# The recurrence's array of terms: from term innermost to key index innermost

## The chip, the cores and the metric

One core of a Trainium2 chip runs the whole program. The time is device time in microseconds (us) of one execution, and the lower the better. Its engines are TensorE (PE: matmuls, with PEld for weight loads), VectorE (DVE), ScalarE (ACT), GpSimd (POOL) and SyncE (SP), which mostly issues DMAs. They run side by side and wait for each other by semaphores.

## What is computed

A block of six parts on 8 sequences of 512 tokens with 128 features: a routed expert layer, six layers of windowed attention, the expert layer again, an attention block with a two-expert mixture, a recurrence over the tokens, and the attention block with its mixture again. The change lies in the recurrence alone. For each batch and each of 16 heads it carries a state `S` of 8 x 8 numbers (key index by value index) through the 512 tokens:

```python
def step(S, inp):
    qt, kt, vt, at, gft = inp
    bs1 = jnp.einsum('bhk,bhkv->bhv', kt, S)
    S1 = S + at[..., :, None] * bs1[..., None, :]
    S2 = jnp.exp(gft)[..., None] * S1
    bs2 = jnp.einsum('bhk,bhkv->bhv', kt, S2)
    S3 = S2 + at[..., :, None] * bs2[..., None, :] + kt[..., :, None] * vt[..., None, :]
    o = jnp.einsum('bhk,bhkv->bhv', qt, S3)
    return (S3, o)
```

Of the outputs `o` only those of the last 176 tokens are used.

## The kernel before

8 batches x 16 heads are 128 states, one on each partition. A state is 8 x 8 float32 words on its partition, value index `v` outside, key index `k` innermost. `SH` is a ring of 8 such states. VectorE runs the recurrence alone, token after token, with the keys, factors and values of 128 tokens (a chunk) in `KW`, `UA`, `FT`, `VT`.

The first 336 tokens, whose outputs nobody asks for, are taken two at a time: `pair`, 168 times. Their new state is the sum of seven 8 x 8 terms: the old state times a factor (term 0), four products of a vector of `UA` with a vector of `Z2` (terms 1 to 4), and two outer products of values and keys (terms 5 and 6). The order on VectorE is: L2808 multiplies the state with four key vectors into `M2`; L2811 writes term 0; L2814 sums `M2` over the key index into `Z2`; L2815 writes terms 5 and 6; L2820 writes terms 1 to 4; L2824 sums the seven terms into the new state in `SH`. The terms lie in `J2` (in the tensor `fw1`), 64 x 7 words with the term innermost.

The other 176 tokens are taken one at a time, with three terms in `MJ` (64 x 3 words, the term innermost): L2875 multiplies the state with two key vectors into `M1`, L2879 makes the state times its factor (`FS`), L2882 sums `M1` into `XY`, L2884 writes term 0 (`FS` plus the outer product `KV`), L2887 writes terms 1 and 2, L2846 (`outer`) prepares the next token's `KV`, and L2895 sums the three terms into the new state. After every 8 tokens L2903 and L2906 make the 8 outputs.

An instruction on VectorE waits for an earlier one only where the program says so (`dve.wait_ge`, or `chain.link`, which waits for the instruction just added): L2814 waits for L2808, L2820 for L2814, L2824 for L2820, and the next step for L2824 (semaphore `R.step`); L2887 waits for L2882, L2895 for L2887 (not for L2846 behind it).

While the pairs run, TensorE and ScalarE work on experts and projections of the later batches. VectorE does small parts for these at fixed tokens of a chunk (`beside`): the bank sum L2731 and statistics L2227 behind tokens 28 and 86, the gates L2748 behind tokens 54 and 108, the key lengths L2754 behind token 123. In the last 176 tokens there is ever less of that, and TensorE comes to rest.

Other lines named below: L2526 to L2529 and L2657 belong to the routing of tokens to experts (`upto` is 8 experts x 32 tiles; L2528 multiplies it with `chosen`, which lies tiles by experts, and L2529 sums it over the experts); L2797 and L2799 belong to the preparation of pairs, and L2799 writes `key[:, :, 0]`, runs of 8 words 16 apart; L1723 on TensorE is the last matmul that L2731 needs.

Of the kernel before, what the change touches and what calls it, by code (L numbers as in the profile page):

```python
# [20 lines left out]
ALU = mybir.AluOpType  # L21
ACT = mybir.ActivationFunctionType
AX_X = mybir.AxisListType.X

P = 128
# [3 lines left out]
HEADS, HD = 16, 8  # L29
# [420 lines left out]
def build(nc, d, out):  # L450
    ctx = ExitStack()
    with ctx:
        def sb(name, shape, dt=F32):
            return ctx.enter_context(nc.sbuf_tensor(name, shape, dt))
# [20 lines left out]
        fw1 = sb("fw1", [P, HID])  # L475
# [37 lines left out]
        at = [0]  # L513

        def take(*shape):
            n = int(np.prod(shape))
            v = arena[:, at[0]:at[0] + n]
            at[0] += n
            assert at[0] <= 34048
            if len(shape) == 2:  # L520
                v = v.rearrange("p (a b) -> p a b", b=shape[1])
            if len(shape) == 3:
                v = v.rearrange("p (a b c) -> p a b c", b=shape[1], c=shape[2])
            return v
# [79 lines left out]
        UA = [take(CH, 2, HD) for _ in range(2)][::-1]  # L604
# [3 lines left out]
        FT, VT = ([take(CH, HD) for _ in range(2)] for _ in range(2))  # L608
        stk, stv, stq, stf = (take(TOKENS) for _ in range(4))
        KV = take(2, HD, HD)  # L610
        FS = take(HD, HD)
        MJ = take(HD * HD, 3)
        SH = take(STEP_RING, HD, HD)
        M1 = take(2 * HD, HD)
        XY = take(2, HD)
# [9 lines left out]
        scaled = [take(TOKENS) for _ in range(2)]  # L625
        N2, RN, T1 = (frow[:, k, :] for k in range(3))
        C1 = LG[:].rearrange("p a b -> p (a b)")[:, 0:CH]
        J2 = fw1[:, 32:32 + 7 * HD * HD].rearrange("p (a r) -> p a r", r=7)
        F2 = OQ.rearrange("p t v k -> p (t v k)").rearrange("p (n k) -> p n k", k=HD)
        at[0] = junk_at  # L630
        K2 = take(CH // 2, 2, HD)
# [4 lines left out]
        Z2 = take(4, HD)  # L636
# [44 lines left out]
        R = RecurrencePhase(sem)  # L681
# [1536 lines left out]
        def _(dve):  # L2218
            chain = Chain(dve, v_chain)
# [515 lines left out]
            def recurrent_experts():  # L2735
# [22 lines left out]
                def prepare(c):  # L2758
                    q = c % 2
                    wide = lambda a: a.unsqueeze(2).broadcast_to([P, R.CHUNK, HD])  # L2760
                    kn, wv, ua, av = KW[q][:, :, 0, :], KW[q][:, :, 1, :], UA[q][:, :, 0, :], UA[q][:, :, 1, :]
                    dve.wait_ge(R.rn_ready, c + 1)
                    chain.link(dve.tensor_tensor(kn, KT, wide(RN), ALU.mult))
                    chain.link(dve.scalar_tensor_tensor(out=av, in0=kn, scalar=-1.0, in1=wide(G1[q]), op0=ALU.mult,
                                                        op1=ALU.mult))
                    chain.add(dve.tensor_tensor(wv, kn, FT[q], ALU.mult))
                    chain.link(dve.tensor_tensor(ua, av, FT[q], ALU.mult))
                    chain.link(dve.tensor_tensor(KT, kn, ua, ALU.mult))
                    chain.link(dve.tensor_reduce(C1, KT, AX_X, ALU.add))
                    chain.link(dve.tensor_tensor(KT, av, wide(C1), ALU.mult))  # L2770
                    chain.link(dve.tensor_tensor(ua, ua, KT, ALU.add))
                    if R.pairs(c):
                        join_pairs(c)
                    dve.engine_nop().then_inc(R.pre_done, 1)
# [28 lines left out]
                def pair(c, at):  # L2803
                    q, n, t = c % 2, at // 2, R.CHUNK * c + at
                    s, new = SH[:, (t - 1) % STEP_RING], SH[:, (t + 1) % STEP_RING]
                    four = [P, 4, HD, HD]
                    dve.wait_ge(R.step, t + 1)
                    chain.add(dve.tensor_tensor(  # L2808
                        M2.rearrange("p (a v) k -> p a v k", a=4), s.unsqueeze(1).broadcast_to(four),
                        KW[q][:, at:at + 2].rearrange("p b a k -> p (b a) k").unsqueeze(2).broadcast_to(four), ALU.mult))  # L2810
                    chain.add(dve.tensor_tensor(J2[:, :, 0].rearrange("p (v k) -> p v k", k=HD), s,  # L2811
                                                F2[:, n].unsqueeze(1).broadcast_to([P, HD, HD]), ALU.mult))
                    dve.wait_ge(v_chain, chain.value() - 1)
                    chain.add(dve.tensor_reduce(Z2.rearrange("p a b -> p (a b)"), M2, AX_X, ALU.add))  # L2814
                    chain.add(dve.tensor_tensor(  # L2815
                        J2[:, :, 5:7].rearrange("p (v k) r -> p r v k", k=HD),
                        VT[q][:, at:at + 2].unsqueeze(3).broadcast_to([P, 2, HD, HD]),
                        K2[:, n].unsqueeze(2).broadcast_to([P, 2, HD, HD]), ALU.mult))
                    dve.wait_ge(v_chain, chain.value() - 1)
                    chain.link(dve.tensor_tensor(  # L2820
                        J2[:, :, 1:5].rearrange("p (v k) r -> p r v k", k=HD),
                        UA[q][:, at:at + 2].rearrange("p b a k -> p (b a) k").unsqueeze(2).broadcast_to(four),
                        Z2.unsqueeze(3).broadcast_to(four), ALU.mult))
                    dve.tensor_reduce(new.rearrange("p v k -> p (v k)"), J2, AX_X, ALU.add).then_inc(R.step, 2)  # L2824

                def beside(c, at):

# [32 lines left out]
                for t in range(TOKENS):  # L2860
                    c, at = divmod(t, R.CHUNK)
                    if at == 0:
                        prepare(c)
                    if at < 2 * R.pairs(c):
                        if at % 2 == 0:
                            pair(c, at)
                        beside(c, at)
                        continue
                    if at == 2 * R.pairs(c):
                        chain.link(outer(t))  # L2870
                    j = t % STEP_RING
                    s = SH[:, (j - 1) % STEP_RING]
                    new = SH[:, j]
                    dve.wait_ge(R.step, t + 1)
                    chain.add(dve.tensor_tensor(  # L2875
                        M1.rearrange("p (a v) k -> p a v k", a=2),
                        s.unsqueeze(1).broadcast_to([P, 2, HD, HD]),
                        KW[c % 2][:, at].unsqueeze(2).broadcast_to([P, 2, HD, HD]), ALU.mult))
                    chain.add(dve.tensor_tensor(  # L2879
                        FS, s, FT[c % 2][:, at].unsqueeze(1).broadcast_to([P, HD, HD]), ALU.mult))  # L2880
                    dve.wait_ge(v_chain, chain.value() - 1)
                    chain.add(dve.tensor_reduce(XY.rearrange("p a b -> p (a b)"), M1, AX_X, ALU.add))  # L2882
                    dve.wait_ge(v_chain, chain.value() - 1)
                    chain.add(dve.tensor_tensor(  # L2884
                        MJ[:, :, 0].rearrange("p (v k) -> p v k", k=HD), FS, KV[:, t % 2], ALU.add))
                    dve.wait_ge(v_chain, chain.value() - 1)
                    chain.add(dve.tensor_tensor(  # L2887
                        MJ[:, :, 1:3].rearrange("p (v k) r -> p r v k", k=HD),
                        UA[c % 2][:, at].unsqueeze(2).broadcast_to([P, 2, HD, HD]),
                        XY.unsqueeze(3).broadcast_to([P, 2, HD, HD]), ALU.mult))  # L2890
                    products = chain.value()
                    if at < last:
                        chain.add(outer(t + 1))
                    dve.wait_ge(v_chain, products)
                    dve.tensor_reduce(new.rearrange("p v k -> p (v k)"), MJ, AX_X, ALU.add).then_inc(R.step, 1)  # L2895
                    if t >= R.QUERIES and j == STEP_RING - 1:
                        if at == j or t == R.QUERIES + j:
                            dve.wait_ge(R.q_in, 32 * (c - 1))
                        seen = slice(t - R.QUERIES - j, t - R.QUERIES + 1)
                        first = max(R.CHUNK * c, R.QUERIES)  # L2900
                        asked = QD[c][:, :, t - j - first:t + 1 - first]
                        dve.wait_ge(R.step, t + 2)
                        chain.link(dve.tensor_tensor(  # L2903
                            OQ, SH, asked.rearrange("p k t -> p t k").unsqueeze(2)
                            .broadcast_to([P, STEP_RING, HD, HD]), ALU.mult))
                        chain.link(dve.tensor_reduce(OD[:, :, seen].rearrange("p v t -> p t v"), OQ, AX_X, ALU.add))  # L2906
                    beside(c, at)
# [16 lines left out]
            for b in range(2):  # L2924
                dve.wait_ge(R.rows_rstd, 1)
                dve.wait_ge(R.y_done, b + 1)
                for i in range(TPB):
                    t = TPB * b + i
# [71 lines left out]
```

## Time and profile before

| | us |
|---|---|
| timed runs, median of 3 | 5263.96 |
| timed runs, lowest to highest | 5259.31 to 5264.52 |
| span of the profiled execution | 5330.8 |

The page gives the profiled execution's own time as its span; it lies 66.8 us above the median of the timed runs. In the rows below, L12 is line 12 of the kernel, an engine's busy time leaves out its waiting, and a duration runs from the start of an instruction to its end, which may lie behind the start of the next one on the same engine. `arena` is the big tile in which most of the named arrays lie (`M2`, `MJ`, `SH`, `KW` and so on), `fw` the one in which `J2` lies.

### The profile page before, as it was taken

The numbers are of one execution on the slowest core, as the hardware profiler recorded it, in microseconds if no ns is written. First come the engines' busy times: TensorE is split into PE (matmuls) and PEld (weight loads), VectorE is DVE, ScalarE is ACT, GpSimd is POOL, SyncE is SP. The second block draws the span as 40 slices with busy tenths as digits, with TensorE's granted clock in tenths as the row PEclk, the third lists the DMA queues.
The fourth block names the chain that finished last, engine by engine and source line by source line (L and its number), as shares of the span: only waits on it lengthen the run. The fifth ranks groups of instructions, "written<-read, shape, count | busy, mean of one in ns | idle before, by whom it ended". The sixth has DMA issues, their size and how long they took to land.

```text
span 5330.8 us, 114063 instructions
## 1 busy us (share of the span) xinstructions
PE 4408.5 (83%) x43126; PEld 2610.7 (49%) x43126; DVE 3292.6 (62%) x14115; ACT 2603.4 (49%) x5100; POOL 1823.8 (34%) x3734
## 2 busy tenths in 40 slices
PE   3779999999999999984669999788770069999999
PEld 3634555555555555543633446455540034446777
DVE  3177777777777777754047772399899957772111
ACT  0336777777777777761324553444440024553333
POOL 3055666666666666662223221000000022220000
PEclk9879999999999999995768998888885568997999
DMA  3600000000000000001511000100100000000000
GB/s 95 163 11 4 2 12 2 2 12 2 6 8 2 12 2 6 2 2 30 165 29 41 1 1 1 25 13 13 31 17 17 0 12 1 1 1 3 5 5 7
DMA packets 125108, 101.75 MB, mean 19 GB/s; under 512 B 22384, under 2 KB 103568, under 8 KB 124560
## 3 DMA queue, kind: packets, MB, share of 16 engines
q1 hardware_dynamic: 119952, 85.00, 5.8%
q0 software_dynamic: 4608, 9.45, 0.8%
q8 instruction: 343, 5.62, 0.4%
q14 instruction: 205, 1.68, 0.1%
HBM read 74.56 MB, written 19.86 MB: 18 GB/s over the span
## 4 chain that ended last, share of the span: by engine, by line
PE 58%; DVE 19%; ACT 7%; POOL 7%; issue 5%; another core or an unknown queue 1%; DMA 1%; SPq 0%; POOLq 0%; DVEq 0%; ACTq 0%; PEldq 0%
PE ps L1746 6%; PE ps L1738 6%; PE ps L1317 5%; PE ps L1357 5%; PE ps L1302 4%; PE ps L1502 4%; PE ps L1514 4%; PE ps L1278 3%; PE ps L1288 3%; PE ps L1543 2%; PE ps L1187 2%; ACT arena L1928 2%; ACT arena L1910 2%; PE ps L1231 2%; DVE arena L2824 2%
## 5 line engine op out<-in xcount | busy, mean ns | idle before, releaser
L2294 DVE CUSTOM_DVE_ANT_0 arena<-ps,mask_win 128x256 f32<-128x256 f32 (+1 forms) x3072 | 1009.3, 387 | 258.5 <-PE ps L1302 256.7
L1910 ACT ACTIVATE arena<-ps 128x512 f32<-128x512 f32 (+1 forms) x1536 | 752.0, 543 | 567.6 <-PE ps L1317 558.5
L1317 PE MATMUL ps<-arena 32*64 32x384 f32 (+2 forms) x6144 | 743.8, 478 | 74.2 <-ACT arena L1910 73.8
L1302 PE MATMUL ps<-arena 32*64 32x192 f32 (+2 forms) x12288 | 696.6, 324 | 14.4 <-DVE arena L2294 13.8
L1746 PEld LDWEIGHTS ps<-w,arena 128*128 128x128 f32 x4096 | 545.1, 195 | 266.3 <-issue 223.4
L2174 ACT ACTIVATE arena<-ps,eb 128x512 f32<-128x512 f32 x512 | 352.2, 689 | 547.0 <-PE ps L1738 546.9
L2467 DVE CUSTOM_DVE_ANT_0 arena<-ps,mask_cau 128x512 f32<-128x512 f32 (+3 forms) x1024 | 446.7, 487 | 255.3 <-PE ps L1502 252.9
L2027 ACT ACTIVATE arena<-ps 128x512 f32<-128x512 f32 (+2 forms) x768 | 363.1, 526 | 463.9 <-PE ps L1514 463.7
L1746 PE MATMUL ps<-w,arena 128*128 128x128 f32 x4096 | 551.7, 279 | 26.4 <-ACT arena L2174 26.4
L990 POOL TENSOR_SCALAR_AFFINE_SELECT arena<-arena 128x1024 f32<-128x1024 f32 x384 | 420.9, 1096 | 395.4 <-ACT arena L1910 393.8
L1738 PE MATMUL ps<-arena,w 128*128 128x512 f32 x1024 | 535.3, 606 | 0.4
L1302 PEld LDWEIGHTS ps<-arena 32*64 32x64 f32 x12288 | 380.7, 134 | 271.1 <-DVE arena L2294 94.5
L1514 PE MATMUL ps<-arena 32*128 32x512 f32 (+2 forms) x1536 | 487.5, 622 | 25.4 <-ACT arena L2027 25.4
L1502 PE MATMUL ps<-arena 32*128 32x512 f32 (+3 forms) x2048 | 426.1, 518 | 22.2 <-DVE arena L2467 16.8
L1357 PE MATMUL ps<-arena 128*32 128x256 f32 (+1 forms) x6144 | 389.0, 372 | 15.4 <-POOL arena L995 15.4
L1042 POOL TENSOR_SCALAR_AFFINE_SELECT arena<-arena 128x512 f32<-128x512 f32 (+1 forms) x192 | 154.3, 805 | 708.8 <-ACT arena L2027 708.4
L2718 DVE SCALAR_TENSOR_TENSOR X<-ps,C,X 128x128 f32<-128x128 f32 x320 | 90.1, 345 | 469.9 <-PE ps L1746 469.9
L995 POOL TENSOR_SCALAR_AFFINE_SELECT arena<-arena 128x1040 f32<-128x1040 f32 (+1 forms) x384 | 343.0, 893 | 26.3
L1187 PE MATMUL ps<-ident,arena 128*128 128x128 f32 x912 | 170.7, 318 | 180.7 <-DVEq L2648 70.3
L955 POOL TENSOR_SCALAR nv<-mv 128x4 f32<-128x4 f32 (+3 forms) x136 | 32.4, 238 | 819.0 <-DVE mv L2231 814.3
L1317 PEld LDWEIGHTS ps<-arena 32*64 32x64 f32 x6144 | 217.6, 133 | 151.0 <-ACT arena L1910 147.4
L1502 PEld LDWEIGHTS ps<-arena 32*128 32x128 f32 x2048 | 192.2, 206 | 184.2 <-issue 82.3
(348 smaller groups left out, 7820.5 us busy)
## 6 DMA issues: line engine op xcount, KB each, us to landing
w<-in_L_w_dram SPq DMA_DIRECT2D x160, 256.0 KB
ys<-arena SPq DMA_DIRECT2D x10, 512.0 KB, 4.4
hs<-arena SPq DMA_DIRECT2D x16, 256.0 KB, 2.3
w<-in_L_w_dram SPq DMA_DIRECT2D x1, 2048.0 KB
scr_k<-arena SPq DMA_DIRECT2D x8, 256.0 KB, 2.3
scr_v<-arena SPq DMA_DIRECT2D x8, 256.0 KB, 2.9
scr_f<-arena SPq DMA_DIRECT2D x8, 256.0 KB, 3.2
arena<-scr_k SPq DMA_DIRECT2D x8, 256.0 KB, 3.6
```

Of the source, the lines that this page charges most:

```text
L990: pool.affine_select(out=a, in_=a, compare_op=ALU.is_ge, fill=0.0, base=0, pattern=[[0, 8], [1, P]], channel_multiplier=-1).then_inc(L.mas ...
L1302: m = pe.matmul(ps[64 * h:64 * h + 64, bank, s.at(v) + lo:s.at(v) + hi], Q[p][r][rows, v, q0:q0 + 64], K[p][r][rows, s.k0 + lo:s.k0 + hi], ...
L1317: m = pe.matmul(out[64 * h:64 * h + 64, :, lo:hi], K[p][r][rows, t.k0 + lo:t.k0 + lo + 64], Q[p][r][rows, 0:2, t.q0 + lo:t.q0 + hi], start ...
L1357: x = pe.matmul(ps[32 * g:32 * g + 32, L.SUMS, t.q0:t.q0 + t.w], Vx[p][:, t.block, at:at + 32], PTs[m % L.SLOTS][:, (2 * k + v) * t.w:(2 * ...
L1502: m = pe.matmul(ps[:, g, s.at(v):s.at(v) + s.kw], Q[p][r][rows, v, s.tile * P:(s.tile + 1) * P], K[p][r][rows, s.k0:s.k0 + s.kw], start=Tr ...
L1514: pe.matmul(ps[:, 4 + k % 2, 0:w].rearrange("p (v q) -> p v q", q=t.w), K[p][r][rows, t.k0:t.k0 + P], Q[p][r][rows, t.vs[0]:t.vs[-1] + 1, ...
L1738: pe.matmul(out if use else out.rearrange("p (i t) -> p i t", t=P), E1(e)[:, c * P:(c + 1) * P], rows(g), start=True, stop=True).then_inc( ...
L1746: m = pe.matmul(ps[:, 2 + e % 2, i * P:(i + 1) * P], hid[c % 2][:, i * P:(i + 1) * P], E2(e)[:, c, :], start=(c == 0 and i == 0), stop=(c ...
L1910: act.activation(PTs[m % L.SLOTS][:, k * w:(k + 1) * w], bank[:, 0:w], exp, scale=-1.0)\
L2027: act.activation(PT[i % 2][:, k * w:(k + 1) * w], ps[:, 4 + k % 2, 0:w], exp, scale=-1.0)\
L2294: x = dve.tensor_tensor_reduce(out=seen, in0=bank[:, s.at(v):s.at(v) + s.kw], in1=mask, scale=1.0, scalar=NO_SCORE, op0=ALU.add, op1=ALU.m ...
L2467: m = dve.tensor_tensor_reduce(out=junk[:, g, s.at(v):s.at(v) + s.kw], in0=ps[:, g, s.at(v):s.at(v) + s.kw], in1=mask, scale=1.0, scalar=N ...
```

## The change

The arrays of terms get the term in the middle and the key index innermost: `MJ` is 8 x 3 x 8 (`v`, term, `k`) instead of 64 x 3, `J2` 8 x 7 x 8 instead of 64 x 7. The products that write the terms run over `v`, term, `k`, so that they write runs of 8 words; before, they wrote words 3 or 7 apart. The sums over the terms read words 8 apart; before, they read the array from end to end. Nothing else is changed: the instructions, their order, their waits and their sizes stay.

```diff
-        MJ = take(HD * HD, 3)
+        MJ = take(HD, 3, HD)
...
-        J2 = fw1[:, 32:32 + 7 * HD * HD].rearrange("p (a r) -> p a r", r=7)
+        J2 = fw1[:, 32:32 + 7 * HD * HD].rearrange("p (v r k) -> p v r k", r=7, k=HD)
...
-                    chain.add(dve.tensor_tensor(J2[:, :, 0].rearrange("p (v k) -> p v k", k=HD), s,
+                    chain.add(dve.tensor_tensor(J2[:, :, 0], s,
                                                 F2[:, n].unsqueeze(1).broadcast_to([P, HD, HD]), ALU.mult))
...
                     chain.add(dve.tensor_tensor(
-                        J2[:, :, 5:7].rearrange("p (v k) r -> p r v k", k=HD),
-                        VT[q][:, at:at + 2].unsqueeze(3).broadcast_to([P, 2, HD, HD]),
-                        K2[:, n].unsqueeze(2).broadcast_to([P, 2, HD, HD]), ALU.mult))
+                        J2[:, :, 5:7],
+                        VT[q][:, at:at + 2].rearrange("p b v -> p v b").unsqueeze(3).broadcast_to([P, HD, 2, HD]),
+                        K2[:, n].unsqueeze(1).broadcast_to([P, HD, 2, HD]), ALU.mult))
                     dve.wait_ge(v_chain, chain.value() - 1)
                     chain.link(dve.tensor_tensor(
-                        J2[:, :, 1:5].rearrange("p (v k) r -> p r v k", k=HD),
-                        UA[q][:, at:at + 2].rearrange("p b a k -> p (b a) k").unsqueeze(2).broadcast_to(four),
-                        Z2.unsqueeze(3).broadcast_to(four), ALU.mult))
-                    dve.tensor_reduce(new.rearrange("p v k -> p (v k)"), J2, AX_X, ALU.add).then_inc(R.step, 2)
+                        J2[:, :, 1:5],
+                        UA[q][:, at:at + 2].rearrange("p b a k -> p (b a) k").unsqueeze(1).broadcast_to([P, HD, 4, HD]),
+                        Z2.rearrange("p a v -> p v a").unsqueeze(3).broadcast_to([P, HD, 4, HD]), ALU.mult))
+                    dve.tensor_reduce(new, J2.rearrange("p v r k -> p v k r"), AX_X, ALU.add).then_inc(R.step, 2)
...
                     chain.add(dve.tensor_tensor(
-                        MJ[:, :, 0].rearrange("p (v k) -> p v k", k=HD), FS, KV[:, t % 2], ALU.add))
+                        MJ[:, :, 0], FS, KV[:, t % 2], ALU.add))
                     dve.wait_ge(v_chain, chain.value() - 1)
                     chain.add(dve.tensor_tensor(
-                        MJ[:, :, 1:3].rearrange("p (v k) r -> p r v k", k=HD),
-                        UA[c % 2][:, at].unsqueeze(2).broadcast_to([P, 2, HD, HD]),
-                        XY.unsqueeze(3).broadcast_to([P, 2, HD, HD]), ALU.mult))
+                        MJ[:, :, 1:3],
+                        UA[c % 2][:, at].unsqueeze(1).broadcast_to([P, HD, 2, HD]),
+                        XY.rearrange("p a v -> p v a").unsqueeze(3).broadcast_to([P, HD, 2, HD]), ALU.mult))
...
-                    dve.tensor_reduce(new.rearrange("p v k -> p (v k)"), MJ, AX_X, ALU.add).then_inc(R.step, 1)
+                    dve.tensor_reduce(new, MJ.rearrange("p v r k -> p v k r"), AX_X, ALU.add).then_inc(R.step, 1)
```

## Rows read from the trace of the kernel before

**Rows 1.** The page: the span, and busy time by engine with its share.
```profile
span 5330.8 us, 114063 instructions
...
PE 4408.5 (83%) x43126; PEld 2610.7 (49%) x43126; DVE 3292.6 (62%) x14115; ACT 2603.4 (49%) x5100; POOL 1823.8 (34%) x3734
```

**Rows 2.** Stretches: length, busy us (instructions) of PE, PEld, DVE, ACT, POOL, granted clock.
```profile
3650.00:3740.00 90.00, 70.80 (x327) 45.94 (x326) 83.24 (x201) 37.65 (x72) 4.12 (x16) 0.83 0.00 1
...
4100.00:4200.00 100.00, 0.00 (x0) 0.00 (x0) 97.34 (x442) 0.00 (x0) 0.00 (x0) 0.50 0.00 0
```

**Rows 3.** Waits of DVE, 3440 to 4310 us: releaser, total us, times, longest.
```profile
DVE arena L2748 <- ACT arena L2155: 8.8, 4, 2.2
...
DVE X L2731 <- PEq L1728: 2.9, 1, 2.9
```

**Rows 4.** The chain that ended last: start us, length, what.
```profile
3505.31 0.88 PE ps L1723 x2
```

**Rows 5.** Timeline of DVE, end of one pair and the next one's start: start, duration.
```profile
3601.62 0.38 DVE L2815 TENSOR_TENSOR fw<-arena 128x128 f32<-128x128 f32 x1
3601.84 0.62 DVE L2820 TENSOR_TENSOR fw<-arena 128x256 f32<-128x256 f32 x1
3602.57 0.62 DVE L2824 TENSOR_REDUCE arena<-fw 128x64 f32<-128x448 f32 x1
3603.22 0.42 DVE L2808 TENSOR_TENSOR arena<-arena 128x256 f32<-128x256 f32 x1
```

**Rows 6.** Timeline of DVE, end of a one-token step and the next one's start.
```profile
4130.52 0.32 DVE L2887 TENSOR_TENSOR arena<-arena 128x128 f32<-128x128 f32 x1
4130.73 0.22 DVE L2846 TENSOR_TENSOR arena<-arena 128x64 f32<-128x64 f32 x1
4130.88 0.35 DVE L2895 TENSOR_REDUCE arena<-arena 128x64 f32<-128x192 f32 x1
4131.26 0.29 DVE L2875 TENSOR_TENSOR arena<-arena 128x128 f32<-128x128 f32 x1
4131.47 0.22 DVE L2879 TENSOR_TENSOR arena<-arena 128x64 f32<-128x64 f32 x1
4131.61 0.28 DVE L2882 TENSOR_REDUCE arena<-arena 128x16 f32<-128x128 f32 x1
```

**Rows 7.** Groups by line, 3440 to 4310 us: count, busy us, mean ns, idle before.
```profile
L2820 DVE TENSOR_TENSOR fw<-arena 128x256 f32<-128x256 f32 x168 | 105.7, 629 | 0.0
L2824 DVE TENSOR_REDUCE arena<-fw 128x64 f32<-128x448 f32 x168 | 104.2, 620 | 17.8 <-DVE fw L2820 0.5
L2808 DVE TENSOR_TENSOR arena<-arena 128x256 f32<-128x256 f32 x168 | 71.7, 426 | 5.3
...
L2895 DVE TENSOR_REDUCE arena<-arena 128x64 f32<-128x192 f32 x176 | 62.1, 353 | 0.1
L2887 DVE TENSOR_TENSOR arena<-arena 128x128 f32<-128x128 f32 x176 | 56.8, 323 | 0.0
...
L2906 DVE TENSOR_REDUCE arena<-arena 128x64 f32<-128x512 f32 x22 | 15.1, 688 | 0.8
```

**Rows 8.** The same view: a product in runs of 8, and one contiguous.
```profile
L2799 DVE TENSOR_TENSOR arena<-arena 128x512 f32<-128x512 f32 x4 | 2.8, 692 | 0.1
L2797 DVE TENSOR_TENSOR arena<-arena 128x512 f32<-128x512 f32 x4 | 2.8, 692 | 0.1
```

**Rows 9.** Groups by line over the whole span: reads with and without a stride.
```profile
L2903 DVE TENSOR_TENSOR arena<-arena 128x512 f32<-128x512 f32 x22 | 22.6, 1027 | 0.9
...
L2528 DVE TENSOR_TENSOR rt<-rt 128x256 f32<-128x256 f32 x2 | 1.2, 618 | 0.1
...
L2657 DVE TENSOR_REDUCE r<-LG 128x32 f32<-128x256 f32 x4 | 1.7, 420 | 0.1
...
L2529 DVE TENSOR_REDUCE arena<-rt 128x32 f32<-128x256 f32 x2 | 1.2, 581 | 0.1
...
L2526 DVE TENSOR_TENSOR rt<-rt,arena 128x256 f32<-128x256 f32 x2 | 0.8, 424 | 0.1
```

## Prediction

> **What bounds the kernel now.** I read the busy time by engine first, then the stretches in which the recurrence runs, then who VectorE waits for in them, then single instructions. Over the whole span TensorE is busiest, at 83% against VectorE's 62% [rows 1], but an edit in one stage is worth what that stage lets through. In the recurrence (about 3,467 to 4,273 us) the picture is another one. In a stretch with two-token steps VectorE is busy 83 of 90 us and TensorE 71; in a stretch with one-token steps VectorE is busy 97 of 100 us and TensorE not at all [rows 2]. VectorE is a serial chain there: a state needs the state before it. So what a step on VectorE gains or loses is nearly all gained or lost at the end.
>
> The exceptions are VectorE's own waits [rows 3]. The one for the bank sum of group 2 (L2731, 2.9 us, once) is a wait for TensorE's own work, and the chain that ended last runs over TensorE until there, at 3,505 to 3,506 us [rows 4]. Up to that point VectorE is ahead by 2.9 us. That point lies behind the pair of tokens 28 and 29, so 15 of the 168 pairs are covered, if the change costs them no more than 2.9 us. The four waits of 2.2 us at L2748 are the second half of a round trip that VectorE itself starts; they move with it and hide nothing. That leaves 153 uncovered pairs and 176 one-token steps.
>
> **The change part by part.** No instruction is added or removed; the same elements are multiplied and summed in the same order of terms. Only strides change.
>
> *The products.* In a pair the three products now write every seventh word; afterwards they write runs of 8. The one that counts is L2820, whose result the sum waits for: 256 elements in 629 ns, where L2808 multiplies the same number into a contiguous tile in 426 ns [rows 7]. That a run of 8 followed by a hop is as good as contiguous is in the trace: L2799 writes 512 elements so and takes 692 ns, as L2797 does contiguously [rows 8]. So the product falls by 203 ns. Behind L2820 there is also a gap of 17.8/168 = 106 ns before the sum starts, where another sum that waits for a product of contiguous writes (L2906 behind L2903) starts after 0.8/22 = 36 ns [rows 7]. I take it that the gap's excess of 70 ns is the tail of scattered writes, and goes too: the gain is 273 ns a pair, with 203 as its lower end.
>
> L2815 and L2811 get shorter too, and this is worth nothing. In the timeline L2820 starts 0.22 us after L2815, though L2815 lasts 0.38 us [rows 5]: scattered writes drain while the next instruction already reads. Only an instruction that waits for the product sees them.
>
> In a one-token step the same holds for L2887 (every third word, 0.32 us). The sum L2895 waits for it, but the outer product L2846 is issued in between, and the sum starts 0.36 us after L2887; the contiguous product L2875 (0.29 us) with the same two behind it has its third start after 0.35 us [rows 6]. The gain is thus about 10 ns a step, at most the 30 ns by which the two products differ. L2884 gains nothing: nobody waits for it alone. If the cover by L2846 were gone, the 30 ns would come in full, 5 us in all.
>
> *The sums.* They read contiguously now: 448 elements in 620 ns (L2824), 192 in 353 ns (L2895) [rows 7]. Afterwards consecutive elements lie 8 words apart. No recurrence sum of the trace does that, so I bound the price x for one element read by the nearest rows [rows 9]. L2528 differs from L2526 in that one operand is read 8 words apart: 618 against 424 ns for 256 elements, x = 0.758 ns. It has the right step, but it is a product. L2529 is a sum that reads 32 words apart: 581 against 420 ns (L2657, contiguous, same size), x = 0.629 ns. It has the right operation, but another step. L2903 reads one operand 48 or 128 words apart: 1027 against the 692 ns of L2797 for 512 elements, x = 0.654 ns. The rows agree within 20%; I take 0.69, between right step and right operation. A slower read holds the engine itself, so unlike the writes it is paid in full, sum for sum: 448 x 0.69 = 309 ns a pair, 192 x 0.69 = 132 ns a step. Nothing covers it: the next step waits for the sum.
>
> *The sum of it all.* 153 x (448x - 273) + 176 x (192x - 10) ns = 102.3x - 43.5 us. At x = 0.69: +27.1 us (5.5 from the pairs, 21.5 from the one-token steps). At 0.629: +20.8. At 0.758: +34.0; with the smaller gains (203 and 0) +46.5. The covered 15 pairs lose 15 x 36 ns = 0.5 us, at the worst ends 2.1 us, which stays within the 2.9 us of the cover. So: the pairs roughly trade a dear product for a dear sum, and the one-token steps, whose product was hardly dear and partly covered, pay almost the whole price of the sum.
>
> The profiled span, 5,330.8 us, is 66.8 us (1.3%) above the median of the timed runs, 5,263.96; the page doesn't say where that lies. My sum is a difference of VectorE intervals. The profiled execution would come to 5,357.9 us by it, and the timed median to 5,263.96 + 27.1 = 5,291 us (scaled by 0.987 the difference would change by 0.4 us, which I neglect).
>
> **The rivals.**
> *A sum reads scattered words for free* (the other side: faster). The place is L2824 and L2895; the mechanism: a sum has one operand and writes one element for 7 or 3 read, so the read side may have time to hop, above all where only three places are visited in turn. Then x = 0 and only the products' gains are left: -43.5 us, or -31.1 with 203 and 0, so 5,220 to 5,233 us. It decides below x = 0.425 ns, where the sum crosses zero. For it: nothing in the rows but the difference in pattern; against it: L2529 is such a sum, with one element written for 8 read, and pays 0.629 ns [rows 9]. The Trainium skill speaks for this rival ("Vector Engine (DVE) Microarchitecture Reference", section 5.2, Measured stream behaviour): beside a loss for a source that hops every element, it reports a one-source operation whose read stream alternated between two far regions, writing one word for two read, at the full rate. By that sentence the change would win; L2529 disagrees for eight places, and no row shows two or three.
>
> *Only the short sum is cheap.* Three places in turn may be free where seven are not: then the 176 steps gain 0 to 10 ns each and the pairs trade evenly, 153 x 36 ns = +5.5 us less 1.8: +4 us, 5,268 us, within the range of no change (from 5,264 to 5,285 by the bounds of the pairs).
>
> *It does not do what it says.* If the scattered writes were not what makes L2820 long, its 273 ns would stay. Its two operands are read in runs or repeated, as L2808's are, and it has the same count of elements, so I see no other cause; the case would cost 153 x 273 ns = 42 us more, 5,333 us.
>
> **How the numbers follow.** Full price as in the rows: 0.70, 5,285 to 5,310 us, likeliest 5,291. Short sum cheap: 0.13, of which a quarter above the bound for slower. Free reads: 0.12, around 5,220 to 5,233. Not doing what it says: 0.01. The remaining 0.04 is for a price between 0.43 and 0.53 ns or somewhat below. A difference under 0.2% (10.5 us, about what a measurement of this kernel can tell from no change) asks for x under 0.53 ns here. So slower 0.73, same 0.13, faster 0.14. The range takes in the first two cases with their bounds: 5,260 to 5,312 us.
>
> **What would show it.** In the changed kernel's profile: L2820 at about 426 ns and the gap before L2824 at about 36 ns; L2824 at 900 to 960 ns instead of 620; L2895 at 475 to 500 instead of 353; L2815 near 292 with the start of L2820 behind it unmoved; the wait at L2731 shorter than 2.9 us by about 0.5. If L2895 stays near 353 ns, the second rival holds; if L2824 stays near 620 too, the first. If L2820 stays near 629, the products were not long for their writes. The prediction is wrong most easily in x, which comes from rows of another step or another operation: 0.1 ns of it is 10 us.

## The result and the profile after

The changed kernel takes 5,271.5 us (median of 12) where the kernel before takes 5,258.4 (median of 12 beside it): a ratio of 1.0026, with a 95% interval of 1.0018 to 1.0034. It is slower by about 13 us, and by 9 to 18 us on the interval. The forecast was slower by 27 us. The direction was right; the loss is half of what I said, and, as the rows show, it lies in the pairs, where I had put a fifth of it.

The groups of VectorE instructions in the recurrence of the changed kernel (count, busy us, mean ns, idle before; they answer to [rows 7]):

```profile
L2824 DVE TENSOR_REDUCE arena<-fw 128x64 f32<-128x448 f32 x168 | 160.8, 957 | 17.7 <-DVE fw L2820 0.5
...
L2820 DVE TENSOR_TENSOR fw<-arena 128x256 f32<-128x256 f32 x168 | 70.1, 417 | 0.0
...
L2895 DVE TENSOR_REDUCE arena<-arena 128x64 f32<-128x192 f32 x176 | 64.2, 365 | 0.1
...
L2887 DVE TENSOR_TENSOR arena<-arena 128x128 f32<-128x128 f32 x176 | 50.1, 284 | 0.0
```

The products fell as they should: L2820 from 629 to 417 ns, L2887 from 323 to 284. The long sum L2824 rose from 620 to 957 ns. The short sum L2895, read with the same step of 8 words, rose only from 353 to 365. And the gap before L2824 did not move: 17.7 us over 168 pairs are 105 ns, as before.

One pair on the timeline of VectorE (start, duration; it answers to [rows 5]), and one one-token step ([rows 6]):

```profile
3528.03 0.28 DVE L2815 TENSOR_TENSOR fw<-arena 128x128 f32<-128x128 f32 x1
3528.23 0.42 DVE L2820 TENSOR_TENSOR fw<-arena 128x256 f32<-128x256 f32 x1
3528.75 0.96 DVE L2824 TENSOR_REDUCE arena<-fw 128x64 f32<-128x448 f32 x1
3529.75 0.42 DVE L2808 TENSOR_TENSOR arena<-arena 128x256 f32<-128x256 f32 x1
...
4060.91 0.28 DVE L2887 TENSOR_TENSOR arena<-arena 128x128 f32<-128x128 f32 x1
4061.11 0.22 DVE L2846 TENSOR_TENSOR arena<-arena 128x64 f32<-128x64 f32 x1
4061.24 0.36 DVE L2895 TENSOR_REDUCE arena<-arena 128x64 f32<-128x192 f32 x1
4061.64 0.29 DVE L2875 TENSOR_TENSOR arena<-arena 128x128 f32<-128x128 f32 x1
```

From L2820's start to the next pair's first product it is 1.52 us now, and was 1.38 [rows 5]; L2820 itself starts 0.02 us sooner behind L2815. From L2887's start to the next step's first product it is 0.73 us, and was 0.74 [rows 6].

Now the total. The view of one line gives its first and last start in the span; here for the two sums, before and after:

```profile
L2824 DVE TENSOR_REDUCE arena<-fw x168: 619/620/622, 3469.0 to 3963.8; 128x64 f32<-128x448 f32 x168
L2895 DVE TENSOR_REDUCE arena<-arena x176: 339/353/355, 3965.6 to 4271.8; 128x64 f32<-128x192 f32 x176
```

```profile
L2824 DVE TENSOR_REDUCE arena<-fw x168: 944/956/975, 3403.5 to 3913.4; 128x64 f32<-128x448 f32 x168
L2895 DVE TENSOR_REDUCE arena<-arena x176: 359/364/375, 3915.5 to 4220.6; 128x64 f32<-128x192 f32 x176
```

The first starts lie 65.5 us apart because the profiled execution of the kernel before, with its span of 5,330.8 us, was slower ahead of the recurrence, in a part that the change does not touch; so only the lengths of the stretches are compared. The pairs take 509.9 us from the first sum to the last, and took 494.8: +15.1. The one-token steps take 305.1 and took 306.2: -1.1. Together +14.0 us, which is the measured 13 us within its interval. By these stretches the whole loss is in the pairs, where I had put 5.5 of 27.1 us; the first two runs below test it.

The pairs themselves lost a little more than 15 us. Over ten undisturbed pairs in a row (no wait and no other work among them) a pair takes 2.520 us after, and 2.408 before: 168 x 112 ns = 18.8 us. Some of it went into waits that VectorE had anyway. The view of [rows 3] has for L2754, before:

```profile
DVE arena L2754 <- ACT arena L2164: 2.1, 1, 2.1
```

And for the changed kernel:

```profile
DVE arena L2748 <- ACT arena L2155: 8.8, 4, 2.2
...
DVE X L2731 <- PEq L1728: 1.3, 1, 1.3
...
DVE arena L2754 <- ACT arena L2164: 0.9, 1, 0.9
```

L2731 waits 1.6 us less, L2754 1.2 us less, and the L2748 waits have not moved at all, as a round trip started by VectorE itself must. 18.8 - 2.8 = 16.0 us against the 15.1 of the stretch.

### The profile page after: what moved, and what is told of

The parts are those of the page before. It is cut to its first block, busy times and chain, and to the rows that moved or that the text cites. A ratio compares the mean times of both kernels' runs of the same rounds, so it can differ in the third digit from the quotient of the medians.

```text
span 5272.2 us, 114063 instructions
## 1 busy us (share of the span) xinstructions
PE 4394.3 (83%) x43126; PEld 2598.3 (49%) x43126; DVE 3311.2 (63%) x14115; ACT 2600.4 (49%) x5100; POOL 1814.2 (34%) x3734
## 4 chain that ended last, share of the span: by engine, by line
PE 59%; DVE 20%; POOL 7%; ACT 7%; issue 5%; DMA 1%; SPq 0%; POOLq 0%; DVEq 0%; ACTq 0%; PEldq 0%
PE ps L1746 6%; PE ps L1738 6%; PE ps L1317 5%; PE ps L1357 5%; PE ps L1302 4%; PE ps L1502 4%; PE ps L1514 4%; PE ps L1278 3%; PE ps L1288 3%; DVE arena L2824 3%; PE ps L1543 2%; PE ps L1187 2%; ACT arena L1928 2%; ACT arena L1910 2%; PE ps L1231 2%
```

## The experiments

Two questions were open: why a step of 8 words costs the sum over seven terms its full price and the sum over three terms next to nothing, and why the gap before L2824 stayed.

**One part at a time.** The first two runs separate the parts of the change: `MJ` and the one-token steps alone, and `J2` and the pairs alone.

```diff
 # e1_steps_only: MJ as in the change, J2 as before
-        MJ = take(HD * HD, 3)
+        MJ = take(HD, 3, HD)
...
 # e2_pairs_only: J2 as in the change, MJ as before
-        J2 = fw1[:, 32:32 + 7 * HD * HD].rearrange("p (a r) -> p a r", r=7)
+        J2 = fw1[:, 32:32 + 7 * HD * HD].rearrange("p (v r k) -> p v r k", r=7, k=HD)
...
```

> Only the one-token steps have the changed layout (MJ); the pairs are as before. Theory (the short sum over 3 terms is nearly free of the read price, the sum over 7 terms pays all of it): L2895 at 365 ns as in the changed kernel, a one-token step as long as before (1.41 us), and the time within 4 us of the kernel before. Rival (the whole change moves the time by something outside these loops): several us slower than before, about half of the 13 us of the full change. The recorded prediction's price (132 ns a step) would give +21 us.

Measured: a ratio of 1.0006 to the kernel before, interval 0.9989 to 1.0024, that is -6 to +13 us; no difference is shown, and the rival's half of 13 us lies inside the interval too. L2895 lasts 366 ns here, and the steps take 305.2 us from first to last sum; the untouched pairs (3395.4 to 3890.2) take 494.8, as in the kernel before:

```profile
L2895 DVE TENSOR_REDUCE arena<-arena x176: 356/366/373, 3892.0 to 4197.2; 128x64 f32<-128x192 f32 x176
```

> Only the pairs have the changed layout (J2); the one-token steps are as before. Theory: the whole loss is here. L2824 at 957 ns against 620 (+337), L2820 at 417 against 629 (-212), the gap before L2824 unchanged at 106 ns: +125 ns a pair, 168 x 125 = +21 us, less about 5 us of waits that VectorE had (2.9 at L2731, 2.1 at L2754): +13 to +17 us against before. Rival (the loss comes half from each part): +6 us.

Measured: a ratio of 1.0040, interval 1.0025 to 1.0055, that is +13 to +29 us, at the centre 21, more than the 13 to 17 expected; the interval overlaps that of the full change (+9 to +18) and leaves out the rival's +6. The pairs take 510.0 us from first to last sum, as in the full change:

```profile
L2824 DVE TENSOR_REDUCE arena<-fw x168: 944/957/979, 3390.7 to 3900.7; 128x64 f32<-128x448 f32 x168
```

So the loss is the pairs', nothing of it is left for the first run's rival, and the recorded price of 132 ns for the short sum is refuted (it would have made +21 us in the first run, beyond its +13).

**What the price of a strided read hangs on.** The two sums differ in three things: how many places they visit in turn (3 or 7), in which tile they read (`arena` or `fw1`), and how far apart the rows of terms are (24 or 56 words). A run with sums added behind the recurrence varies these one by one:

```diff
 # e3_sums_measured, behind the recurrence; flat = the 512 words of OQ; each line three times
+ deep = lambda r, w, s=None: (flat if s is None else s)[:, 0:HD * r * w].rearrange('p (v r k) -> p v k r', r=r, k=w)[:, :, 0:HD]
+ chain.link(dve.tensor_reduce(out64, flat[:, 0:192].rearrange('p (a r) -> p a r', r=3), AX_X, ALU.add))   # L2919
...
+ chain.link(dve.tensor_reduce(sq, deep(2, 8), AX_X, ALU.add))        # L2923, then r = 3 to 8 up to L2935
+ chain.link(dve.tensor_reduce(sq, deep(3, 8, J2f), AX_X, ALU.add))   # L2937; r = 4 L2939, r = 7 L2941
+ chain.link(dve.tensor_reduce(sq, deep(3, 9), AX_X, ALU.add))        # L2943; steps of 12 L2945, 16 L2947
...
```

> The changed kernel with a series of sums added on VectorE behind the recurrence, each waiting for the one before it, so the time is longer by their own length and only their durations count. They sum r terms over 64 results, from OQ in the arena (r = 2 to 8, terms 8 words apart; r = 3 and 7 also contiguous; other steps of 9, 12, 16 and 64 words) and from J2 (r = 3, 4, 7). Theory A (few places in turn are free): in both tiles r = 3 lasts about 365 ns and r = 7 about 957 ns, and somewhere in r = 4 to 6 the price sets in; other steps change little. Rival B (the place decides: J2 lies in another tile than MJ): r = 7 from OQ about 620 ns, r = 3 from J2 about 490 ns. Rival C (the step between terms or between rows decides): r = 3 with steps of 9, 12 or 16 words or with terms 64 words apart about 490 ns. Three short groups at the end test the gap of 106 ns before L2824: a 256-element product and the sum that waits for it, alone, with a 128-element product right ahead of it, and the same with the strided sum. If the gap is made by the instruction ahead, it is about 36 ns in the first group and 106 in the others; if it belongs to reading J2, it is 106 in all three.

Measured (groups by line; the count of input elements is 64 times the number of terms):

```profile
L2935 DVE TENSOR_REDUCE arena<-arena 128x64 f32<-128x512 f32 x3 | 3.2, 1066 | 0.1
L2941 DVE TENSOR_REDUCE arena<-fw 128x64 f32<-128x448 f32 x3 | 2.8, 947 | 0.1
...
L2933 DVE TENSOR_REDUCE arena<-arena 128x64 f32<-128x448 f32 x3 | 2.8, 945 | 0.1
...
L2949 DVE TENSOR_REDUCE arena<-arena 128x64 f32<-128x448 f32 x3 | 2.8, 937 | 0.1
L2953 DVE TENSOR_REDUCE arena<-arena 128x64 f32<-128x448 f32 x3 | 2.7, 905 | 0.1
L2931 DVE TENSOR_REDUCE arena<-arena 128x64 f32<-128x384 f32 x3 | 2.5, 832 | 0.1
...
L2929 DVE TENSOR_REDUCE arena<-arena 128x64 f32<-128x320 f32 x3 | 2.2, 720 | 0.1
...
L2939 DVE TENSOR_REDUCE arena<-fw 128x64 f32<-128x256 f32 x3 | 1.8, 605 | 0.1
L2927 DVE TENSOR_REDUCE arena<-arena 128x64 f32<-128x256 f32 x3 | 1.8, 603 | 0.1
...
L2943 DVE TENSOR_REDUCE arena<-arena 128x64 f32<-128x192 f32 x3 | 1.1, 378 | 0.1
L2925 DVE TENSOR_REDUCE arena<-arena 128x64 f32<-128x192 f32 x3 | 1.1, 373 | 0.1
L2937 DVE TENSOR_REDUCE arena<-fw 128x64 f32<-128x192 f32 x3 | 1.1, 373 | 0.1
L2951 DVE TENSOR_REDUCE arena<-arena 128x64 f32<-128x192 f32 x3 | 1.1, 372 | 0.1
...
L2919 DVE TENSOR_REDUCE arena<-arena 128x64 f32<-128x192 f32 x3 | 1.1, 353 | 0.1
...
L2923 DVE TENSOR_REDUCE arena<-arena 128x64 f32<-128x128 f32 x3 | 0.9, 286 | 0.1
```

Read from below: two terms 286 ns (a contiguous sum of 128 elements, L2882, takes 279); three terms 373 against 353 contiguous (L2919); four terms 603, where a contiguous sum of 256 takes 420 [rows 9]. Between three and four the price jumps from 0.1 to 0.71 ns an element and then stays: at seven it is (945 - 620) / 448 = 0.73, and the sums of five, six and eight (720, 832, 1066) lie on the same line. The tile makes no difference (L2937 and L2939 and L2941 read `J2` in `fw1`: 373, 605, 947). Nor does the step make much: for three terms 9 words give 378 ns, 12 and 16 words 369 and 368, and terms 64 words apart (L2951) 372; for seven, 9 words give 937 (L2949) and 64 words still 905 (L2953). Theory A holds, rivals B and C fall.

The three groups for the gap showed about 35 ns each (a product starts at 4254.17 and lasts 0.42 us, its sum starts at 4254.63), also with another product right ahead. So neither what is ahead of the product nor reading `J2` makes the 106 ns; both expectations for the gap missed.

**Whole pairs, and runs instead of steps.** The next run puts copies of whole pairs behind the recurrence, to find the gap and to see whether products too are free at two places in turn.

```diff
 # e4_pairs_measured, the fifth series (halves, the term innermost, rows of 7 words), h = 0 and 1
...
+ chain.add(dve.tensor_tensor(J2f.rearrange('p (v k r) -> p v k r', r=7, k=HD)[:, :, :, 1 + 2 * h:3 + 2 * h],
+           U4[:, 2 * h:2 * h + 2].rearrange('p a k -> p k a').unsqueeze(1).broadcast_to([P, HD, HD, 2]),
+           Z2[:, 2 * h:2 * h + 2].rearrange('p a v -> p v a').unsqueeze(2).broadcast_to([P, HD, HD, 2]), ALU.mult))
...
 # the seventh: one product of four terms, rows of 8 words
+ chain.link(dve.tensor_tensor(flat.rearrange('p (v k r) -> p v k r', r=8, k=HD)[:, :, :, 0:4], ...
```

> The changed kernel with seven series of whole pairs added on VectorE behind the recurrence (4 each, written to spare places, so that the state is not touched); only their durations and gaps count. The first repeats a pair of the changed kernel, with the sum over 7 terms at about 957 ns and a gap of 106 ns before it. Second: the wait ahead of L2820's copy is moved ahead of L2815's copy. Third: L2815's copy is left out. Fourth: the four products go to another tile (M2) than the sum reads. Theory (the gap comes from the instruction ahead of the product being still under way when the product starts, with a wait in between): 36 ns in the third, 106 in the first and fourth. Rival (the gap belongs to a sum that reads what the product has just written): 36 in the fourth alone. Fifth to seventh: with the term innermost again the four products are written in runs: as two products of two terms each (runs of 2 words, 7 apart, then 8 apart), and as one product of four terms (runs of 4 words, 8 apart), whose operands are then read at 2 or 4 places in turn. Theory A (up to three places in turn are free, more are not): a product of two terms about 290 ns, as a contiguous one; the product of four terms 600 to 620. Rival D (only a sum, with its one operand and its few writes, reads three places for free): a product of two terms 370 ns or more.

Measured. The products (L2963 and L2964 are the halves with rows of 7 words, L2973 one with rows of 8, L2983 the product of four terms, L2928 the changed kernel's):

```profile
L2983 DVE TENSOR_TENSOR arena<-arena 128x256 f32<-128x256 f32 x4 | 2.3, 581 | 0.0
...
L2928 DVE TENSOR_TENSOR fw<-arena 128x256 f32<-128x256 f32 x4 | 1.7, 419 | 0.0
...
L2963 DVE TENSOR_TENSOR fw<-arena 128x128 f32<-128x128 f32 x4 | 1.2, 306 | 0.0
...
L2964 DVE TENSOR_TENSOR fw<-arena 128x128 f32<-128x128 f32 x4 | 1.2, 290 | 0.0
L2973 DVE TENSOR_TENSOR arena<-arena 128x128 f32<-128x128 f32 x4 | 1.2, 288 | 0.0
```

A product that reads both operands at two places in turn and writes runs of two words lasts 288 to 306 ns, as a contiguous one (292); at four places 581 instead of 419, (581 - 419) / 256 = 0.63 ns an element. So theory A, as far as two places and four, holds for products as well, and rival D falls. Where the runs of two words start, on rows of 7 or of 8 words, hardly matters.

The gap is about 35 ns in every series, the copy of the pair included (timeline of the first series):

```profile
4220.32 0.42 DVE L2928 TENSOR_TENSOR fw<-arena 128x256 f32<-128x256 f32 x1
4220.77 0.95 DVE L2929 TENSOR_REDUCE arena<-fw 128x64 f32<-128x448 f32 x1
```

0.45 us from start to start, where the loop has 0.52. Both theories of the gap that I had put down fall. The copy differs from the pair in the loop in one point of the program: its sum adds 1 to `v_chain`, the loop's adds 2 to `R.step`. It also runs while the other engines rest. The next run but one tells these apart.

**A faster pair.** If two places are free, the scattered writes can be avoided without a strided sum: keep the old array, and write the four products in two instructions of two terms, in runs of two words.

```diff
 # e5_two_products, on the kernel before
-                    chain.link(dve.tensor_tensor(
-                        J2[:, :, 1:5].rearrange("p (v k) r -> p r v k", k=HD),
...
+                    for h in range(2):
+                        chain.add(dve.tensor_tensor(
+                            J2[:, :, 1 + 2 * h:3 + 2 * h].rearrange("p (v k) r -> p v k r", k=HD),
+                            UA[q][:, at + h].rearrange("p a k -> p k a").unsqueeze(1).broadcast_to([P, HD, HD, 2]),
+                            Z2[:, 2 * h:2 * h + 2].rearrange("p a v -> p v a").unsqueeze(2).broadcast_to([P, HD, HD, 2]),
+                            ALU.mult))
+                    chain.join()
```

> The kernel before, with one change: L2820's four products are made by two instructions of two terms each, written with the term innermost (runs of 2 words) into the old array, so that the sum reads from end to end. If reading two places in turn and writing runs of two words are free (theory A), a half lasts about 290 ns, the second starts 0.21 us behind the first, and the sum starts about 0.61 us behind the first instead of 0.735: 125 ns a pair, over the 153 pairs not covered -19 us against the kernel before, -17 to -21 with the waits at the ends of chunks. If the products pay for their places (rival D), a half lasts 380 ns or more and the second waits behind the first: 0 to +10 us.

Measured: a ratio of 0.9981 to the kernel before, interval 0.9967 to 0.9996: 2 to 17 us faster, at the centre 10, less than the 17 to 21 expected. The halves are near what they should be (L2821, 302 ns), and a pair lasts 2.28 us instead of 2.41. But the pairs together take 479.4 us from first to last sum instead of 494.8: 15.4 us less, and not the expected 168 x 125 ns = 21, because VectorE now waits 7.0 us at L2731 (2.9 before) and 4.6 at L2754 (2.1).

```profile
L2827 DVE TENSOR_REDUCE arena<-fw x168: 619/620/622, 3400.8 to 3880.2; 128x64 f32<-128x448 f32 x168
...
L2821 DVE TENSOR_TENSOR fw<-arena 128x128 f32<-128x128 f32 x336 | 84.0, 302 | 0.0
...
DVE X L2731 <- PEq L1728: 7.0, 3, 4.9
DVE arena L2754 <- ACT arena L2164: 4.6, 2, 3.0
```

**The gap.** On the kernel before, the pair's sum adds 1 to `R.step`, and the waits are renumbered.

```diff
 # e6_count_by_one
+    def steps(self, t):
+        return t // 2 if t < self.QUERIES else t - self.QUERIES // 2
...
-                    dve.wait_ge(R.step, t + 1)
+                    dve.wait_ge(R.step, R.steps(t) + 1)
...
-                    dve.tensor_reduce(new.rearrange("p v k -> p (v k)"), J2, AX_X, ALU.add).then_inc(R.step, 2)
+                    dve.tensor_reduce(new.rearrange("p v k -> p (v k)"), J2, AX_X, ALU.add).then_inc(R.step, 1)
```

> The kernel before, with one change: the sum of a pair adds 1 to the semaphore of the steps instead of 2, and all who wait for it count accordingly. Theory (the 106 ns before L2824 come from its adding 2, since the same pair with a sum that adds 1 to another semaphore showed 36 ns): the gap falls to about 36 ns, a pair from 2.40 to 2.33 us, 153 x 70 ns = -10.7 us against before, -8 to -11 with the waits at the ends of chunks. Rival (the gap comes from the other engines being busy while the pairs run, as they were not behind the recurrence): the gap stays at 106 ns and the time is the same.

Measured: a ratio of 0.9978, interval 0.9964 to 0.9991; 5 to 19 us faster. The idle time before the sum (now L2827) falls from 17.8 to 5.8 us, 35 ns a pair, with the writes of the product (now L2823) as scattered as ever:

```profile
L2823 DVE TENSOR_TENSOR fw<-arena 128x256 f32<-128x256 f32 x168 | 105.5, 628 | 0.0
L2827 DVE TENSOR_REDUCE arena<-fw 128x64 f32<-128x448 f32 x168 | 104.2, 620 | 5.8
```

So the gap came from adding 2, and not from the busy engines around it. The page of this run's profile shows what it came with:

```profile
span 5257.9 us, 113895 instructions
...
PE 4402.7 (84%) x43126; PEld 2598.3 (49%) x43126; DVE 3295.7 (63%) x14115; ACT 2602.7 (50%) x5100; POOL 1818.2 (35%) x3734
```

There are 168 instructions fewer than before [rows 1], one for each pair, though the counts of the five engines' busy instructions are the same. In the trace's records the sum that adds 1 holds its own wait for the product. The sum that adds 2 holds none: ahead of it stands a semaphore instruction of 21 ns on VectorE, left out of the views above, that does the waiting, and the sum starts 43 ns after that one's end. By these records what costs the 70 ns is the wait in an instruction of its own; that a larger addition is slower in itself is not shown.

**Both together.** The edits of the last two runs in one kernel, e7_two_products_by_one.

> The kernel before with the four products in two instructions (as in e5_two_products) and the sum adding 1 to the semaphore (as in e6_count_by_one). Theory: both gains add on VectorE, 125 + 70 = 195 ns a pair, so a pair lasts 2.21 us; of 168 x 195 = 33 us only a part arrives, since VectorE then waits longer for TensorE and ScalarE (L2731, L2754): -13 to -20 us against before. Rival: no gain beyond the 10 us of e5_two_products, since the waits take up all the rest.

Measured: 5,241.9 us against 5,258.8, a ratio of 0.9968, interval 0.9955 to 0.9982: 9 to 24 us faster than the kernel before. That is the lowest ratio of the three, but their intervals overlap. The gap is 35 ns and the halves 302 ns; a pair lasts 2.21 us. Of 168 x 195 ns = 33 us the stretch of the pairs keeps 22 in the profile (its sums start from 3397.5 to 3870.3, that is 472.8 us against 494.8), and some 17 are measured at the end; the wait of L2731, now L2734, has grown to 10.8 us, and that of L2754, now L2757, to 5.9:

```profile
L2830 DVE TENSOR_REDUCE arena<-fw 128x64 f32<-128x448 f32 x168 | 104.2, 620 | 5.8
L2824 DVE TENSOR_TENSOR fw<-arena 128x128 f32<-128x128 f32 x336 | 83.9, 302 | 0.0
...
DVE X L2734 <- PEq L1731: 10.8, 4, 6.1
...
DVE arena L2757 <- ACT arena L2167: 5.9, 2, 3.7
```

## Why the prediction was right in direction and wrong in size

- *What bounds.* Right. VectorE's chain sets the recurrence's length, and the loss of the stretch (+14.0 us) is, within the interval, the loss at the end (+13). The cover at L2731 shrank from 2.9 to 1.3 us and was not used up. I had left out L2754, which hid another 1.2 us.
- *The product L2820.* Right: 629 to 417 ns, predicted 426. L2815 and L2811 got shorter for next to nothing, as said: 0.02 us a pair at most.
- *The gap before L2824.* Wrong. I took its 70 ns of excess for the tail of scattered writes and booked them as a gain, 153 x 70 ns = 10.7 us. It stayed, because it comes from the sum's adding 2 to its semaphore, which puts the wait into an instruction of its own (e6_count_by_one). The sum I had compared it with, L2906, differed in the product's writes and in its semaphore, and I saw only the first. The lower end, 203 ns a pair, was the right one.
- *The long sum.* Right within a tenth: 337 ns more, predicted 309. x is 0.75 in the loop, the value of the row with the same step of 8 words.
- *The short sum.* Wrong, and the larger error: 12 ns more, predicted 132, so 176 x 120 ns = 21 us of loss that did not come. The step that failed is the use of one price x for both sums. The rows it came from all visit many places in turn: L2528 32, L2529 8, L2903 8. The price is not one for the step; it sets in between three and four places (e3_sums_measured). The second rival, "only the short sum is cheap", held; I gave it 0.13, since the rows I had showed no read at three places. It put the time at 5,268 us, and with the upper end of x and the lower end of the product's gain at up to 5,285; measured were 5,271.5.
- *The sum.* The errors partly cancelled: the pairs were underrated by some 10 us, the steps overrated by 22. That the direction came out right was in part luck: four fifths of the forecast loss were the short sum's, which lost nothing, and had the gap gone as forecast, the pairs would have lost only about 4 us (15.1 - 10.7).
- *The Trainium skill.* The statement that I weighed for the first rival ("Vector Engine (DVE) Microarchitecture Reference", section 5.2, Measured stream behaviour) is that a one-source operation whose read stream alternated between two regions ran at the full read rate. The trace agrees for two terms: 286 ns here, 279 for a contiguous sum of as many elements. The statement covers two regions only; that three cost little (373 ns) and four the full price (603 ns) is what the runs here add. Against the rival I had set L2529, a row with eight places, and it says nothing of two or three.

What makes three places nearly free and four not was not tried: the runs show where the border lies, not what in the engine draws it. Products were measured at two and at four places, not at three.

## What to carry to other kernels

A strided read had no single price here: count how many places the read stream visits in turn, and take the price from a row with that count. Changing a layout moves the stride from the write to the read, so ask which of the two waits for the other, and whether a third order (here runs of two words on both sides) has neither. And compare a gap only with one whose waits and semaphore updates are the same, and count the instructions of the whole span: an instruction that no view lists can stand in it.

## What the runs showed of the hardware

- In float32 sums of 64 results VectorE reads two or three places in turn at nearly the full rate (0.05 and 0.1 ns more an element), and four, seven or eight at 0.71 to 0.74 ns more with a step of 8 words (three, four and seven in either of two tiles). Seven places cost 0.71 with a step of 9 words and 0.64 with one of 64 (e3_sums_measured).
- A product that reads both operands at two places in turn lasts as long as a contiguous one (288 to 306 against 292 ns for 128 elements); at four places it pays 0.63 ns an element (e4_pairs_measured).
- Scattered writes (every seventh word) add about 0.8 ns an element to the instruction (629 against 417 ns for 256), but they hardly hold up the next one that doesn't wait for them: L2820 starts 0.22 us behind L2815 where that lasts 0.38, and 0.20 us behind it where it lasts 0.28.
- A sum that adds 2 to a semaphore instead of 1 has its wait in a semaphore instruction of its own, and starts 70 ns later: 106 against 35 ns behind the product that it waits for. In this kernel that was worth 5 to 19 us (e6_count_by_one).
